# Moving a bias add from the front to the experts' splits, with another order of steps around it

## The reference, cut to what matters

```python
x = _layernorm(x, norm_g, norm_b)                       # over the 256 features
se = _layernorm(slot_embeds, slot_g, slot_b) * scale    # 16 experts x 64 slots
logits = einsum('bnd,esd->bnes', x, se)
dispatch = softmax(logits, axis=1)                      # over the tokens
combine = softmax(logits.reshape(B, N, -1), axis=-1)    # over the slots
slots = einsum('bnd,bnes->besd', x, dispatch)
gate = gelu(einsum('besd,edf->besf', slots, Wg) + bg)
up = einsum('besd,edf->besf', slots, Wu) + bu
eout = einsum('besf,efo->beso', gate * up, Wd) + bd
y = einsum('bns,bso->bno', combine, eout)
```

## Time and profile before

| | us |
|---|---|
| median of 3 runs | 1256.28 (1252.44 to 1260.27) |
| profiled execution, its own time | 1263.61 |
| its span, first to last instruction | 1261.9 |
| PE busy | 1170.2 (93%) |
| DVE busy | 802.1 (64%) |
| ACT busy | 667.1 (53%) |
| POOL busy | 585.4 (46%) |
| mean granted PE clock | 0.968 |

### The profile page before, as it was taken

The page is one execution under the profiler, slowest core; times in us unless marked ns, Lnnn a source line. Parts: engine busy times, 40 slices in busy tenths (PEclk is TensorE's granted clock), DMA queues, the critical chain, the costliest instruction groups (busy, mean ns, idle before and its releaser), DMA issues.

```text
span 1261.9 us, 19086 instructions
## 1 busy us (share of the span) xinstructions
PE 1170.2 (93%) x6838; PEld 915.0 (73%) x6870; DVE 802.1 (64%) x1266; ACT 667.1 (53%) x930; POOL 585.4 (46%) x400
## 2 busy tenths in 40 slices
PE   6699999999999999988699999967999999999996
PEld 5466766676766666646578777756888888889885
DVE  5767777868686868646877777845445444532344
ACT  2545556565656565557477777743555555541112
POOL 6455565655556565323466666633544444430000
PEclk9889999999999999979899999978999999999998
DMA  4645545454545455601143335336555545553771
GB/s 136 143 101 120 135 98 130 128 134 126 139 120 135 127 121 129 183 4 68 38 145 117 118 117 176 100 101 196 176 175 175 167 153 152 160 201 113 233 246 62
DMA packets 126670, 170.29 MB, mean 135 GB/s; under 512 B 47041, under 2 KB 77186, under 8 KB 126594
## 3 DMA queue, kind: packets, MB, share of 16 engines
q1 hardware_dynamic: 124498, 168.74, 46.0%
q10 hardware_dynamic: 2096, 0.56, 0.2%
HBM read 72.26 MB, written 37.75 MB: 87 GB/s over the span
## 4 chain that ended last, share of the span: by engine, by line
PE 71%; DVE 15%; ACT 5%; issue 4%; SPq 1%; DMA 1%; POOL 1%; ACTq 0%; DVEq 0%; POOLq 0%
PE ring L431 9%; PE ring L433 8%; PE ring L432 8%; PE ring L1571 7%; PE ring L1421 6%; PE tail L1432 6%; PE ring L1406 6%; PE tail L431 3%; PE tail L432 3%; PE tail L433 3%; DVE sls L1232 3%; PE tail L1392 2%; PE tail L1571 2%; PE ring L1454 2%; ACT x L856 2%
## 5 line engine op out<-in xcount | busy, mean ns | idle before, releaser
L1121 DVE TENSOR_REDUCE mx<-ring 128x4 f32<-128x512 f32 (+2 forms) x192 | 200.0, 1044 | 89.1 <-PE ring L1408 83.5
L837 ACT ACTIVATE pt<-ring 128x1024 f32<-128x1024 f32 (+1 forms) x192 | 168.6, 880 | 109.8 <-PE ring L1421 85.4
L699 POOL TENSOR_SCALAR_AFFINE_SELECT pt<-pt 128x512 f32<-128x512 f32 x128 | 84.9, 664 | 175.2 <-ACT pt L837 174.8
L1406 PE MATMUL ring<-qks 96*128 96x384 f32 (+3 forms) x512 | 139.7, 361 | 7.3 <-DMA qks<-stg 4.7
L1421 PE MATMUL ring<-qks 98*128 98x256 f32 (+3 forms) x512 | 139.8, 376 | 7.1 <-DVE mx L1121 6.6
L716 POOL TENSOR_TENSOR dl<-e,dh 128x1024 fp32r<-128x1024 f32 x32 | 76.6, 2404 | 128.5 <-ACT e L908 128.5
L1421 PEld LDWEIGHTS ring<-qks 98*128 98x128 f32 x512 | 79.5, 194 | 75.4 <-issue 39.6
L740 POOL TENSOR_TENSOR hl<-hid,hh 128x512 fp32r<-128x512 f32 x64 | 82.6, 1301 | 78.1 <-ACT hh L943 78.1
L1432 PE MATMUL tail<-pt,va 128*32 128x512 f32 (+3 forms) x1024 | 97.5, 454 | 7.7 <-issue 4.9
L1242 DVE SCALAR_TENSOR_TENSOR hid<-ring,bias_e,gate 128x512 f32<-128x512 f32 x64 | 47.8, 748 | 84.7 <-ACT gate L937 53.2
L1406 PEld LDWEIGHTS ring<-qks 96*128 96x128 f32 x512 | 91.4, 197 | 13.4 <-issue 5.7
(11 more groups left out here) (239 smaller groups left out, 3154.5 us busy)
## 6 DMA issues: line engine op xcount, KB each, us to landing
qks<-stg SPq DMA_DIRECT2D x384, 128.0 KB, 2.4
c_dram<-c2s SPq DMA_DIRECT2D x32, 512.0 KB, 4.7
c<-c_dram SPq DMA_DIRECT2D x32, 512.0 KB, 6.2
sl_dram<-sls SPq DMA_DIRECT2D x32, 256.0 KB, 3.4
wg<-in_wg SPq DMA_DIRECT2D x16, 512.0 KB, 5.6
wu<-in_wu SPq DMA_DIRECT2D x16, 512.0 KB, 6.1
wd<-in_wd SPq DMA_DIRECT2D x16, 512.0 KB, 6.9
sl<-sl_dram SPq DMA_DIRECT2D x16, 512.0 KB, 4.6
```

The source lines that it names most:

```text
L699: nc.gpsimd.affine_select(out=m, in_=m, compare_op=ALU.is_ge, fill=0.0, base=0, pattern=[[0, GH], [1, P]], channel_multiplier=-1).then_inc ...
L837: nc.scalar.activation(pt[j % 2][:, h:h + heads, 0:n], heads_of(tile, heads, n), ACT.Exp, scale=SCALE).then_inc(empty, 1)
L1121: nc.vector.tensor_reduce(out=mx[:, g, h:h + heads, i], in_=heads_of(tile, heads, (i + 1) * P), axis=AX.X, op=ALU.max).then_inc(empty, 1)
L1406: nc.tensor.matmul(scores[:, h, :], qks[0:KS_ROWS, g, 0, h0 + h, i * P:(i + 1) * P], qks[0:KS_ROWS, g, 1, h0 + h, 0:n], start=(h == k), st ...
```

## The change

1. In the front the two L1232 instructions of each `slots` step are gone, and with them the link between them and L1228. `CHAIN`, the count of such links, changes with it (B * NT to B * 2).
2. In the splits of the slots (k = 0) ACT now makes `slh` with an Identity activation that adds `nb_`, once for each half of the features (128x512), and DVE makes `sll` as (sl + nb_) - slh with two scalar_tensor_tensor instructions.
3. The steps of the front stand in another order on PE, ACT and POOL; DVE's and SP's rounds are kept.
4. The last batch has another order on PE, ACT and DVE. ACT's `weight` steps, which stood first, come behind the `e` pairs.
5. The seam counts are new. Worked out, `zT 0` comes right after `exp 7,2,5` on PE (5 steps earlier); on ACT `xn 0` and `zh 0` come one to three steps earlier, `s1 0,1` behind `yTT 7`, and `apply 7` a round later (after `sumB 1,0`); on SP `z 0` and `z 1` come earlier, `store 6` after `c2 0,3` and `store 7` after `z 3`. `ln 7` on DVE keeps its place.

```diff
--- before.py
+++ after.py
@@ -95,33 +95,33 @@
 
 
 PE_FRONT = (
-    ("sumT", -1, 1), ("topT", 0), ("c2", 0, 0), ("zT", 1), ("sumB", -1, 1), ("topB", 0), ("slots", -1, 1), ("s1", 1, 0), ("c2", 0, 1),
-    ("c2", 0, 2), ("s1", 1, 1), ("sumT", 0, 0), ("s1", 1, 2), ("s1", 1, 3), ("sumB", 0, 0), ("slots", 0, 0), ("c2", 0, 3),
+    ("sumT", -1, 1), ("topT", 0), ("c2", 0, 0), ("zT", 1), ("c2", 0, 1), ("topB", 0), ("sumB", -1, 1), ("slots", -1, 1), ("s1", 1, 0),
+    ("c2", 0, 2), ("c2", 0, 3), ("s1", 1, 1), ("sumT", 0, 0), ("s1", 1, 2), ("s1", 1, 3), ("sumB", 0, 0), ("slots", 0, 0),
 )
 ACT_FRONT = (
-    ("c2", 0, 0), ("sumB", -1, 1), ("xn", 1), ("e", 0, 0), ("e", 0, 1), ("e", 0, 2), ("zh", 1), ("c2", 0, 1), ("s1", 1, 0), ("e", 0, 3),
-    ("c2", 0, 2), ("s1", 1, 1), ("s1", 1, 2), ("s1", 1, 3), ("sumB", 0, 0), ("c2", 0, 3),
+    ("c2", 0, 0), ("c2", 0, 1), ("xn", 1), ("e", 0, 0), ("e", 0, 1), ("sumB", -1, 1), ("zh", 1), ("e", 0, 2), ("c2", 0, 2), ("s1", 1, 0),
+    ("c2", 0, 3), ("e", 0, 3), ("s1", 1, 1), ("s1", 1, 2), ("s1", 1, 3), ("sumB", 0, 0),
 )
 DVE_FRONT = (
     ("sumT", -1, 1), ("topT", 0), ("zT", 1), ("sub", 0, 0), ("sub", 0, 1), ("xn", 1), ("sub", 0, 2), ("sub", 0, 3), ("slots", -1, 1),
     ("s1", 1, 0), ("s1", 1, 1), ("sumT", 0, 0), ("s1", 1, 2), ("s1", 1, 3), ("rows", 1), ("slots", 0, 0),
 )
 POOL_FRONT = (
-    ("lo", 0, 0), ("lo", 0, 1), ("sum", 0, 0), ("lo", 0, 2), ("lo", 0, 3), ("zl", 1), ("sum", 0, 1),
+    ("lo", 0, 0), ("lo", 0, 1), ("sum", 0, 0), ("lo", 0, 2), ("zl", 1), ("lo", 0, 3), ("sum", 0, 1),
 )
 SP_FRONT = (("c2", 0, 0), ("c2", 0, 1), ("slots", -1, 1), ("z", 2), ("slots", 0, 0), ("c2", 0, 2), ("c2", 0, 3))
 
 PE_LAST = (
-    ("topT", 0), ("c2", 0, 0), ("topB", 0), ("sumT", -1, 1), ("slots", -1, 1), ("sumB", -1, 1), ("c2", 0, 1), ("slots", 0, 0),
-    ("sumT", 0, 0), ("sumB", 0, 0), ("slots", 0, 1), ("sumT", 0, 1), ("c2", 0, 2), ("sumB", 0, 1), ("c2", 0, 3),
+    ("topT", 0), ("c2", 0, 0), ("sumT", -1, 1), ("topB", 0), ("sumB", -1, 1), ("slots", -1, 1), ("c2", 0, 1), ("slots", 0, 0),
+    ("sumT", 0, 0), ("sumB", 0, 0), ("c2", 0, 2), ("c2", 0, 3), ("slots", 0, 1), ("sumT", 0, 1), ("sumB", 0, 1),
 )
 ACT_LAST = (
-    ("weight", 0, 3), ("weight", 0, 1), ("c2", 0, 0), ("e", 0, 0), ("e", 0, 1), ("e", 0, 2), ("c2", 0, 1), ("sumB", -1, 1),
-    ("weight", 0, 2), ("e", 0, 3), ("sumB", 0, 0), ("c2", 0, 2), ("sumB", 0, 1), ("weight", 0, 0), ("c2", 0, 3),
+    ("c2", 0, 0), ("e", 0, 0), ("e", 0, 1), ("sumB", -1, 1), ("e", 0, 2), ("c2", 0, 1), ("e", 0, 3), ("weight", 0, 1), ("sumB", 0, 0),
+    ("weight", 0, 2), ("c2", 0, 2), ("weight", 0, 3), ("c2", 0, 3), ("sumB", 0, 1), ("weight", 0, 0),
 )
 DVE_LAST = (
-    ("topT", 0), ("sub", 0, 0), ("sub", 0, 1), ("sumT", -1, 1), ("sub", 0, 2), ("sub", 0, 3), ("weight", 0, 3), ("slots", -1, 1),
-    ("sumT", 0, 0), ("slots", 0, 0), ("sumT", 0, 1), ("slots", 0, 1), ("weight", 0, 1), ("weight", 0, 0),
+    ("topT", 0), ("sumT", -1, 1), ("sub", 0, 0), ("sub", 0, 1), ("sub", 0, 2), ("sub", 0, 3), ("slots", -1, 1), ("sumT", 0, 0),
+    ("slots", 0, 0), ("weight", 0, 1), ("weight", 0, 3), ("sumT", 0, 1), ("slots", 0, 1), ("weight", 0, 0),
 )
 POOL_LAST = (
     ("lo", 0, 0), ("lo", 0, 1), ("sum", 0, 0), ("lo", 0, 2), ("lo", 0, 3), ("sum", 0, 1),
@@ -129,10 +129,10 @@
 SP_LAST = (("weight", 0, 1), ("weight", 0, 2), ("weight", 0, 3), ("slots", -1, 1), ("slots", 0, 0), ("weight", 0, 0), ("weight", 1, 0),
            ("c2", 0, 0), ("c2", 0, 1), ("c2", 0, 2), ("c2", 0, 3), ("slots", 0, 1))
 
-PE_JOIN = (12, 6, 3, 2, 1)
-ACT_JOIN = (7, 2, 2, 2, 1, 1, 1, 1, 1, 1, 1, 1, 1, 1, 1, 1, 1, 1, 1, 1, 1)
-DVE_JOIN = (4, 4, 4, 2, 2, 2, 1, 1, 1, 1, 1, 1, 1, 1, 1)
-SP_JOIN = (2, 1, 1, 1, 1, 1, 1, 1)
+PE_JOIN = (17, 5, 3, 2, 1)
+ACT_JOIN = (8, 5, 2, 1, 1, 1, 1, 1, 1, 1, 1, 1, 1, 1, 1, 1, 1, 1, 1, 1, 1, 1, 1, 1, 1, 1, 1, 1, 1, 1, 1, 1, 1, 1, 1, 1, 1)
+DVE_JOIN = (5, 4, 3, 2, 2, 2, 1, 1, 1, 1, 1, 1, 1, 1, 1)
+SP_JOIN = (4, 3, 2, 2, 2, 2, 2, 2, 1, 1, 1, 1)
 POOL_JOIN = ()
 
 PAIR_STEPS = ("lat", "max", "exp", "v", "yTT", "cproj", "wv", "seT", "zT", "s1", "topT", "topB", "sumT", "sumB", "c2", "slots")
@@ -404,7 +404,7 @@
     POOL_SETUP = 10
     IN_LAT, IN_SMALL, IN_ROPE, IN_SG, IN_SE, IN_TAIL = 5, 7, 2, 3, 1, 4
     ATTN_CHAIN, COMBINE_CHAIN = G + G + 3 + 1 + 3 * NEWTON, 13
-    CHAIN = B * ATTN_CHAIN + B * NT
+    CHAIN = B * ATTN_CHAIN + B * 2
 
     cos2, sin2 = (bcast(t[:, :].unsqueeze(1), [P, 2, T]) for t in (cos, sin))
 
@@ -767,7 +767,12 @@
             def split_high(p, i, k):
 
                 act.wait_ge(w_loaded[i][k], (p + 1) * 16)
-                nc.scalar.activation(highs[i][k][:, :, :], raw[i][k][:, :, :], ACT.Copy).then_inc(w_high, 1)
+                if k == 0:
+                    for c in range(NC):
+                        last = nc.scalar.activation(slh[i][:, c, :], sl[i][:, c, :], ACT.Identity, bias=nb_[:, c:c + 1])
+                else:
+                    last = nc.scalar.activation(highs[i][k][:, :, :], raw[i][k][:, :, :], ACT.Copy)
+                last.then_inc(w_high, 1)
 
             for st in order(ACT_AT, ACT_FRONT, ACT_LAST, ACT_JOIN):
                 name, b = st[:2]
@@ -1027,8 +1032,13 @@
 
             def split_low(p, i, k):
                 dve.wait_ge(w_high, (2 * p + i) * 4 + (FIRST_SPLITS.index(k) if first(p) and i == 0 else k) + 1)
-                nc.vector.tensor_tensor(out=lows[i][k][:, :, :], in0=raw[i][k][:, :, :], in1=fp(highs[i][k][:, :, :]),
-                                        op=ALU.subtract).then_inc(w_low, 1)
+                if k == 0:
+                    for c in range(NC):
+                        last = nc.vector.scalar_tensor_tensor(out=sll[i][:, c, :], in0=sl[i][:, c, :], scalar=nb_[:, c:c + 1],
+                                                              in1=fp(slh[i][:, c, :]), op0=ALU.add, op1=ALU.subtract)
+                else:
+                    last = nc.vector.tensor_tensor(out=lows[i][k][:, :, :], in0=raw[i][k][:, :, :], in1=fp(highs[i][k][:, :, :]), op=ALU.subtract)
+                last.then_inc(w_low, 1)
 
             for st in order(DVE_AT, DVE_FRONT, DVE_LAST, DVE_JOIN):
                 name, b = st[:2]
@@ -1227,9 +1237,6 @@
                     for d in range(NC):
                         last = nc.vector.scalar_tensor_tensor(out=sls[h][:, d, :], in0=tile[:, d, :], scalar=ng[:, d:d + 1], in1=sls[h][:, 1, :],
                                                               op0=ALU.mult, op1=ALU.mult)
-                    blink(last)
-                    for d in range(NC):
-                        last = nc.vector.tensor_scalar(out=sls[h][:, d, :], in0=sls[h][:, d, :], scalar1=nb_[:, d:d + 1], scalar2=None, op0=ALU.add)
                     last.then_inc(empty, 1)
                 elif name == "weight":
                     split_low(0, b, st[2])
```

## The result

The changed kernel takes 1225.8 us (median of four runs, 1224.7 to 1228.91) against 1256.05 before; the ratio of the runs is 0.976, with a 95% interval of 0.973 to 0.980. Forecast were 1225.0 us and a range of 1216 to 1239.

The account below looks back on a forecast made before the run. PE's own work was taken to bound rounds and experts, with waits to win in the rounds and last batch. -13.9 - 17.7 + 0.3 = -31.3 us, from the median of 1256.28 to 1225.0 us; range 1216 to 1239.

Parts of the forecast that it names:

- The rounds: Six rounds of the front: 30.0 us each, 180.0 against 193.95, so -13.9 us.
- The floor of 29.85 us: PE's own steps in one front round, set end to end: 29.85 us, the least that any order can take.
- the schedule that found no wait: New order of a front round: every PSUM tile and input is in time for PE, the closest by 0.4 us.
- GpSimd's hold on L1232: Front rounds: the bias add of twice 0.45 us lasts 3.82 us, its first instruction returning when GpSimd's 2.53 us add ends.
- The last batch: From the first slots of batch 6 to gate_up: 33.2 us instead of 50.92, so -17.7 us.
- e0: ScalarE's first `e` pair in the last batch, right behind c2 and ahead of the weight steps: forecast at 827.6.
- The seam: First round and seam: +0.3 us, bounds -9.6 and +2; PE's 9.64 us wait for the layernorm chain stays.
- The splits: Slots splits in two halves: expert 0's counted in the last batch, the other 15 on half idle engines, 0 us.
- rival D: Experts: a GpSimd instruction slips between the halves of sll in each of 15 experts, 36 us, 1261; chance 0.05.
- B: Rival, front rounds: lo goes ahead of xnl, s1,0 starts 1 us later, 6 us in all, 1231; chance 0.14.
- C: Rival, last batch: part of the stall stays through late weights or a stretched GpSimd chain, +7 us, 1232; chance 0.14.
- E: Rival, first round: GpSimd's new order leaves the layernorm chain a gap, up to 9.6 us more go, 1216; chance 0.07.

Follow-up runs that it names:

- free_pair: Changed kernel plus, in L1232's place in each slots step, a link and two VectorE instructions reading PSUM that add nothing to sls; 1238.74 us, ratio 0.987.
- bias_only: Changed kernel with all step orders and seam counts of before, so only the bias moves into the splits; 1238.46 us, ratio 0.984.
- ln_later_slh_first: ln_later with ScalarE's and VectorE's splits of expert 0's slots one step earlier in the last batch; 1215.17 us, ratio 0.969.
- weights_first: Changed kernel with ScalarE's three weight splits of expert 0 back at the head of the last batch; 1236.99 us, ratio 0.984.
- order_only: Kernel of before with the orders and seam counts of the changed kernel, the bias (L1232) staying in the front; 1242.58 us, ratio 0.988.
- old_seam: Changed kernel with the seam counts (JOIN lines) of before; 1224.55 us, ratio 0.974.
- ln_later: Changed kernel with VectorE's layernorm chain of batch 7 (ln 7) behind rows 1 instead of behind s1 1,0; 1219.26 us, ratio 0.969.

## Why the prediction was right

| term | forecast | first profile of before | second profile of before |
|---|---|---|---|
| six rounds | -13.9 | -15.3 | -15.4 |
| last batch | -17.7 | -16.4 | -17.7 |
| last cproj to first slots | +0.3 with the seam | -1.0 | -0.6 |
| start, attention with the seam | in the term above | -6.4 | +3.6 |
| experts and combination | 0 | +0.3 | -0.3 |
| span | -31.3 | -38.9 | -30.4 |

That 1225.8 came so near to 1225.0 is in part luck: the rounds gave 1.4 us more than forecast and the seam about 1 us more, the last batch 1.3 us less by the first profile, and the runs of before alone are spread over 7.8 us.

*The rounds.* The floor of 29.85 us and the schedule that found no wait are borne out: 29.77 us a round and no wait of PE in the list. The 0.15 us that I added for starts after a semaphore was too much; with PE busy for 178.62 of 178.62 us there were none. What the forecast put down to GpSimd's hold on L1232 is, by free_pair, at least 0.97 us of the 2.18 us a round that the bias costs in the new order; up to 1.21 is the link and the pair themselves. The sum did not depend on this. The prediction also read the earlier trace rows wrongly in one point: it has the first of the two L1232 come back when L721 ends. The longest single one lasts 2.58 us, so that the other took 1.3 of the 3.82:

```profile
L1232 DVE TENSOR_SCALAR sls<-sls,nb__52 x32: 474/489/2580, 628.3 to 868.6; 128x512 f32<-128x512 f32 x32
```

```profile
701.32 4.79 POOL L716 TENSOR_TENSOR dl<-e,dh 128x1024 fp32r<-128x1024 f32 x2 [10.84 <-ACT e L908]
```

The first came back about when this lo ended (706.11), the second when L721 ended (708.61): both were held. It was also not the order that won here: five rounds of bias_only last 29.77 us with the old order. The forecast asked only whether the new order reaches the floor, and never set the old one without L1232 beside it.

*The last batch.* The chain that I wrote out is the one that ran, step for step; set back by the 22.80 us between the cuts, sll was forecast to end at 830.8 and ended at 832.3. The 1.4 us gathered on the way: e0 0.3 us late, slots 7,0 begun 0.4 late, slots 7,1 full 0.9 late, and drained 1.6 late, behind sumT, sumB and `sls`; sll and gate_up gave 0.2 back. The two biased activations took 1.33 us instead of my estimate of 1.15, but ended at 830.68, before VectorE was free. The forecast also set the last batch at the length that PE's steps have in a round (5.6 us a slots step) without saying why the low clock of before should go; it went, and that is 5.7 us of the 16.4. That the queues and not sl's load end last is shown by ln_later_slh_first, where ScalarE and VectorE split the slots one step earlier and gate_up came 0.95 us earlier. The weight steps' place is worth 11.6 us by weights_first, near the 12.5 us of the earlier trace rows; order_only's last batch, with L1232 in it, is 5.7 us longer than the changed one.

*The seam.* Forecast +0.3 with bounds of -9.6 and +2; the measured -0.6 to -1.0 after the last cproj lie within, but on the other side of nothing, and old_seam shows about 1 us. Whether attention itself moves by a microsecond with the seam can't be told, since it varies by 6.

*The splits.* In the experts, nothing, as forecast. The new pairs (min/median/max of one), VectorE and ScalarE:

```profile
L1037 DVE SCALAR_TENSOR_TENSOR sll<-sl,nb__52,slh x32: 741/748/754, 830.9 to 1068.8; 128x512 fp32r<-128x512 f32 x32
```

```profile
L772 ACT ACTIVATE slh<-sl,nb__52 x32: 707/712/716, 829.4 to 1067.4; 128x512 fp32r<-128x512 f32 x32
```

No sll instruction was held (maximum 754 ns), but that is no answer to rival D: in neither trace does a split of the slots overlap a GpSimd instruction, so the case that D supposes never came up. What does meet is the next pair, wgl on VectorE and wul on GpSimd. In one expert of the changed kernel:

```profile
871.01 1.21 DVE L1040 TENSOR_TENSOR wgl<-wg,wgh 128x1024 fp32r<-128x1024 f32 x1
871.63 2.85 POOL L732 TENSOR_TENSOR wul<-wu,wuh 128x1024 fp32r<-128x1024 f32 x1 [4.28 <-ACT wuh L774]
```

Where wul starts near the end of wgl it lasts 2.50 us, here 2.85, and up to 3.25 where it starts earlier in it: GpSimd waits for VectorE this time. Its mean goes from 2555 ns to 2775 by more such meetings (beside wdl for expert 0, 3.38 us), but it is 2593 in bias_only with the same splits, so this is the order and the moment, not the two halves of sll. PE's time in the experts has not changed (264.96 us busy, 264.80 in the earlier trace rows).

*The other rivals.* B (xnl caught by lo): no wait for it in any round. C: the weights were in time. E (the layernorm chain gets free) did not happen by the change, since GpSimd's stretch has no gap there; its mechanism was right, and ln_later collects 8.4 us of the 9.6 that it was priced at by placing the chain elsewhere.

## What to carry to other kernels

Where engines run written-out queues, set the steps of a period end to end on the busiest one and ask of each whether its tile and inputs are there; do it for the old order too with the disputed instruction left out, or the order gets the credit of the instruction. A step that waits for a transfer belongs as late in its queue as its use allows: three splits at the head of a queue cost 11.6 us here, and behind the exponentials ScalarE had no wait for them. A short chain of small VectorE instructions on SBUF should be put where GpSimd is idle, even if that is later.

## What was not expected

- A VectorE instruction can be short in work and long in stand-off: 8 columns took 2.31 us beside GpSimd's 2.4 us instructions and 0.17 us after them (ln_later). In the same place a 128x512 instruction lasted at most 0.69 us with one input in PSUM (free_pair), and up to 2.63 us as a tensor_scalar on SBUF alone (order_only). The Trainium skill (SBUF — State Buffer, Who interferes with whom) has a VectorE instruction with two SBUF inputs, and tensor_scalar in a two-port mode, contend with GpSimd, and one with at most one SBUF input outside these modes not. The runs agree, as far as the operands go; no trace names the mode of L1232.
- A link and a pair in VectorE's queue, never held, still cost 1.21 us a round and 5.6 us in the last batch, where PE waits for them at topB, at c2,3 and ahead of gate_up, one after another (4.0 us), and works slower by 1.6 us.
- Two executions of the same kernel differed by 4.2 us at the first cproj and by 5.8 us from there to the last, and the first pair of profiles was off by 8.6 us from the difference of the medians; stretches cut at instructions agreed to 0.1 us in the rounds (193.95 and 194.03) and 1.3 us in the last batch.
